# Attention with keys in tiles of 128: scores in four narrow matmuls, and half of the steps from kept score pieces that a transposing DMA turns

## The chip, the cores and the metric

One core of a Trainium2 chip runs the whole program. The metric is the device time of one execution in microseconds (us). The median of three runs of the kernel before is 2221.08 us (2217.85 to 2222.08).

## The reference

Two layers act on x of shape (4, 256, 64, 64), that is 4 batches of 256 channels by 4096 positions. Each adds its result to x and normalises its own input by groups of 8 channels first.

```python
# layer 0, on xn = group_norm(x), xf = xn as (B, 256, 4096)
f = einsum('kc,bcn->bkn', Wq, xf) + bq      # 32 channels
g = einsum('kc,bcn->bkn', Wk, xf) + bk      # 32 channels
h = einsum('oc,bcn->bon', Wv, xf) + bv      # 256 channels
s = einsum('bki,bkj->bij', f, g)            # 4096 x 4096
beta = softmax(s, axis=1)                   # over i
x = x + gamma * einsum('bci,bij->bcj', h, beta)
# layer 1, on group_norm(x)
y = relu(bn(W1 x))                          # 32 channels
z = relu(bn(W2 packed(y_i * y_j)))          # 528 pair products to 256 channels
x = x + z
```

The softmax runs over i, the positions of f (called queries in the kernel); j, the positions of g, are called keys. Every number goes through the array as float16 in a high and a low part, so one product of two split operands takes three matmuls: high by high, high by low, low by high.

## The kernel before

**Tiles.** A batch has 32 key tiles of 128 (NT) and 8 chunks of 512 queries (NCH). There are two kinds of score matmul. A piece (`step_piece`, line 1546) holds the scores of one key tile by one chunk with the keys on the partitions, in PSUM bank `tps[0]`; VectorE takes its maximum over the queries (line 801). There are 8 pieces for a key tile, 1024 in all. A step (line 1565) holds scores with the queries on the partitions: 128 queries by 512 keys (one group G), written as one matmul of 512 columns to one of two banks `sps`. The negated maxima of the group enter as three extra rows of `gst` (96 to 98): VectorE reduces them (`tile_max`), GpSimd splits them in three (`split_max`, eight small instructions, lines 1130 to 1137), TensorE turns them with four matmuls of 128 columns (`rows`, line 1572), ScalarE copies them to `gst` (`row_copy`, line 1293).

**A step** u is made in this order. TensorE writes the scores two steps ahead. ScalarE takes the exponential twice, once to float16 (`ph`, line 1300, three slots) and once to float32 (`p32`, line 1303, two slots). VectorE subtracts (`pl`, line 842). TensorE then runs 12 matmuls: for each of four key subtiles `ph` by `hth` (line 1758, 257 columns, the last one sums the powers), `ph` by `htl` (line 1759, 256 columns) and `pl` by `hth` (line 1766, 257 columns). Each subtile has its own bank `acc[0..3]`, which accumulates over the 32 steps of its group. The piece of the step 40 pieces ahead stands between the high and the low part.

**Kept steps.** From the third group of batch 0 on, one step in eight (step 4 of each eight) is kept: ScalarE copies a piece from PSUM to `ks` (line 1310), VectorE takes its maximum there (line 816) and makes a bias, ScalarE takes the exponential of `ks` twice with that bias (lines 1317, 1318), GpSimd subtracts (`kept_low`, line 1121), and a DMA issued by SP turns high and low part into `kt` (line 474). TensorE uses `kt` in lines 1725, 1726 and 1729 and needs no scores for that step. There are 120 kept and 904 made steps.

**Around it.** At the end of a group VectorE takes reciprocals of the sums and divides two of the four subtiles, ScalarE divides the other two (line 1323), and TensorE turns the result at steps 4 and 7 of the next group (`transposed`, line 1580). From batch 1 on the second layer of the batch before is woven into the steps: `rest_of_z` at step 0 of a group (7 matmuls of 512 columns, lines 1616, 1618, 1613), then ScalarE's `z_out` (line 1357) and `product_high` (line 1349), GpSimd's `low` (1098), `value_bias` (1112), `product` (1142) and `residual` (1148). Between batches `values` makes `hth` and `htl`. Ahead of the first step a prologue, in the order of the table `ORDER`, makes queries, keys and values of batch 0 and 40 pieces. The tail behind the last step is the rest of layer 1.

**Order.** Nothing is planned at run time: every engine runs its own program in order, and semaphores hold the engines together. So a wait in one engine's list also holds what stands behind it there.

Of the kernel before, what the change touches and what calls it, by code (L numbers as in the profile page):

```python
# [16 lines left out]
P = 128  # L17
CH = 512
# [14 lines left out]
KEPT_FROM = 2  # L33
KEPT = 1
TURNS_OF = (1, 2, 3, 4, 5, 0, 6, 7)
PLACES = (5,)
KEPT_STEPS = (4,)
LO = 2.0 ** 11
EXP_SHIFT = 8.0
SLOTS = 3  # L40
# [11 lines left out]
def build(nc, x, wq, wk, wv, w1, w2, vec, ident, gmean, sel, out):  # L52
# [5 lines left out]
    with ctx:  # L58
# [22 lines left out]
        p32 = sb("p32", [P, 2, CH], f32)  # L81
        ph = sb("ph", [P, SLOTS, CH], f16)
        pl = sb("pl", [P, SLOTS, CH], f16)
        mx = sb("mx", [P, NT, NCH], f32)
        nm = sb("nm", [P, QT], f32)
        mw = sb("mw", [P, 7, QT], f32)
        r1 = sb("r1", [P, QT], f32)
        r2 = sb("r2", [P, QT], f32)
        r3 = sb("r3", [P, QT], f32)
        mrow = sb("mrow", [P, QT, P], f16)  # L90
        ks = sb("ks", [P, KEPT, CH], f32)
        kb = sb("kb", [P, KEPT, 2, CH], f16)
        kt = sb("kt", [P, QT, KEPT, 2 * QT, P], f16)
        kn = sb("kn", [P, 1], f32)
        kbias = sb("kbias", [P, 1], f32)
# [61 lines left out]
        tps = [ctx.enter_context(nc.psum_tensor(f"tps{i}", [P, CH], f32)) for i in range(2)]  # L157

# [18 lines left out]
        t_mm = [sem("t_mm0"), sem("t_mm1")]  # L177
        t_free = [sem("t_free0"), sem("t_free1")]
# [9 lines left out]
        kx_ok, kn_ok, kbias_ok = sem("kx_ok"), sem("kn_ok"), sem("kbias_ok")  # L188
        kp_ok, kl_ok = sem("kp_ok"), sem("kl_ok")
        kt_in = [sem(f"kt_in{i}") for i in range(KEPT)]  # L190
        acc_mm = sem("acc_mm")
        rinv_ok = sem("rinv_ok")
        ot_act = sem("ot_act")
        ot_dve = sem("ot_dve")
# [127 lines left out]
        def z_half(n, h):  # L322

            if n >= SHARED:
                return zt[set_of(n)][:, h]
            return {(SHARED - 2, 1): p32[:, 1], (SHARED - 1, 0): ks[:, 0],
                    (SHARED - 1, 1): p32[:, 0]}.get((n, h), zt0[:])

        def rows_of(grp):
# [4 lines left out]
        ORDER = (("x", 0), ("x", 1), ("x", 2), ("qk", 0), ("x", 3), ("v", 0, 0), ("v", 0, 1), ("max", 2), ("qk", 1),  # L334
# [7 lines left out]
        AHEAD = len(EARLY)  # L342
        ALL = B * NT * NCH

        FIRST_TILE = KEPT_FROM * QT
        TILES = B * NT
        kept_fill = {}

# [1599 lines left out]
```

## Time and profile before

| | |
|---|---|
| median of three runs | 2221.08 us (2217.85 to 2222.08) |
| span of the profiled execution | 2216.6 us |
| TensorE busy | 2164.2 us, 98% |
| VectorE busy | 1857.5 us, 84% |
| ScalarE busy | 1734.7 us, 78% |
| GpSimd busy | 801.5 us, 36% |
| first attention matmul starts at | 87.7 us |

Busy time counts an instruction from its start to its modelled end, and neighbours overlap: a matmul of 257 columns is shown with 0.27 us, but one starts every 0.11 us. So for a price the start-to-start distance in the timeline is read, not the duration. The same holds for the other engines to a smaller degree (an exponential is shown with 0.69 us and the next one starts 0.57 us after it). In timeline rows an "x4" stands for four instructions merged, and the time beside it runs from the first start to the last end.

### The profile page before, as it was taken

What the parts mean: (1) busy time and instruction counts of PE and PEld (TensorE: products, weight loads), DVE (VectorE), ACT (ScalarE), POOL (GpSimd) and SP (SyncE); (2) the same over time, 40 slices, a digit from 0 to 9 for tenths busy, and PEclk for the clock granted to TensorE, in tenths of its full rate; (3) what the DMA queues carried; (4) which work ended last, traced back from release to release, by engine and by line L of the source; (5) the groups of instructions that cost most, each with busy time, mean ns of one, the idle gap of its engine ahead of it and who ended that gap; (6) DMA issues with size and microseconds to landing.
All of it is one profiled execution on the core that took longest, in us unless ns stands there. A gap on an engine that the chain in (4) does not pass through costs nothing.

```text
span 2216.6 us, 43342 instructions
## 1 busy us (share of the span) xinstructions
PE 2164.2 (98%) x16662; PEld 1607.4 (73%) x16662; DVE 1857.5 (84%) x3220; ACT 1734.7 (78%) x2806; POOL 801.5 (36%) x832
## 2 busy tenths in 40 slices
PE   4899999999999999999999999999999999999999
PEld 3577777777777777777777777777787777777754
DVE  7788888878888888888888898888988888888677
ACT  5578888878777788888777788888877778777777
POOL 2111222223233443453533344444344333343346
PEclk9999999999999999999999999999999999999999
DMA  6001111111123333322233233333212222122212
GB/s 198 14 6 20 20 26 23 27 28 28 31 60 89 82 89 80 82 64 71 62 81 85 65 83 88 89 79 85 62 35 58 61 59 53 34 50 52 62 35 76
DMA packets 186957, 132.58 MB, mean 60 GB/s; under 512 B 135520, under 2 KB 142432, under 8 KB 186720
## 3 DMA queue, kind: packets, MB, share of 16 engines
q1 hardware_dynamic: 186752, 129.81, 23.7%
q8 instruction: 132, 2.16, 0.4%
q14 instruction: 73, 0.60, 0.1%
HBM read 71.83 MB, written 19.92 MB: 41 GB/s over the span
## 4 chain that ended last, share of the span: by engine, by line
PE 90%; DVE 5%; ACT 2%; issue 1%; DMA 1%; POOL 0%; SPq 0%; ACTq 0%; POOLq 0%; DVEq 0%
PE acc L1766 16%; PE acc L1758 16%; PE acc L1759 16%; PE tps L1546 9%; PE sps L1565 8%; PE tps L1616 3%; PE acc L1540 3%; PE acc L1729 2%; PE acc L1725 2%; PE acc L1726 2%; PE tps L1618 2%; DVE mx L801 2%; PE acc L1616 1%; PE tps L1580 1%; DVE pl L842 1%
## 5 line engine op out<-in xcount | busy, mean ns | idle before, releaser
L1300 ACT ACTIVATE ph<-sps,esc 128x512 f16<-128x512 f32 x904 | 619.9, 686 | 318.7 <-PE sps L1565 312.7
L1758 PE MATMUL acc<-hth,ph 128*128 128x257 f16 x3488 | 814.7, 274 | 1.0 <-ACT ot L1323 0.9
L1759 PE MATMUL acc<-htl,ph 128*128 128x256 f16 x3488 | 813.4, 273 | 0.0
L801 DVE TENSOR_REDUCE mx<-tps 128x1 f32<-128x512 f32 x904 | 617.9, 686 | 224.4 <-PE tps L1546 214.1
L842 DVE TENSOR_TENSOR pl<-p,ph 128x512 f16<-128x512 f32 x904 | 737.3, 818 | 65.5 <-ACT p L1303 63.1
L1303 ACT ACTIVATE p<-sps,esc 128x512 f32<-128x512 f32 x904 | 616.8, 682 | 0.0
L1766 PE MATMUL acc<-hth,pl 128*128 128x257 f16 x3488 | 527.9, 273 | 0.0
L1766 PEld LDWEIGHTS acc<-hth,pl 128*128 128x128 f16 x3488 | 340.5, 98 | 134.6 <-issue 0.3
L1759 PEld LDWEIGHTS acc<-htl,ph 128*128 128x128 f16 x3488 | 341.4, 98 | 117.2 <-issue 0.3
L1546 PE MATMUL tps<-fst,gst 96*128 96x512 f16 x1024 | 390.7, 383 | 16.1 <-DVE mx L801 11.0
L1758 PEld LDWEIGHTS acc<-hth,ph 128*128 128x128 f16 x3488 | 341.1, 98 | 57.4 <-ACT ot L1323 2.7
L1121 POOL TENSOR_TENSOR kb<-ks,kb 128x512 f16<-128x512 f32 x120 | 149.0, 1241 | 596.2 <-ACT ks L1318 596.2
L1565 PE MATMUL sps<-gst,fst 128*128 128x512 f16 x904 | 343.1, 380 | 0.5 <-ACT p L1303 0.5
L1098 POOL TENSOR_TENSOR xl<-xn,xh 128x512 f16<-128x512 f32 x176 | 224.9, 1297 | 275.3 <-DVE xn L782 251.1
L1142 POOL TENSOR_TENSOR rt<-rt,yb 128x512 f32<-128x512 f32 (+1 forms) x120 | 179.0, 1523 | 42.4 <-DMA rt<-turned 42.2
L1546 PEld LDWEIGHTS tps<-fst,gst 96*128 96x128 f16 x1024 | 100.0, 98 | 50.5 <-DVE mx L801 25.5
L1130 POOL TENSOR_TENSOR r<-nm,mw 128x4 f32<-128x4 f32 x32 | 17.8, 555 | 307.7 <-DVE nm L837 307.7
L1725 PE MATMUL acc<-hth,kt 128*128 128x257 f16 x480 | 111.9, 274 | 0.0
L1726 PE MATMUL acc<-htl,kt 128*128 128x256 f16 x480 | 111.8, 273 | 0.0
L1262 ACT ACTIVATE xh<-xb,nbias,rstd 128x512 f16<-128x512 f32 x136 | 102.6, 806 | 9.3 <-DVE nbias L621 9.3
L1565 PEld LDWEIGHTS sps<-gst,fst 128*128 128x128 f16 x904 | 88.6, 98 | 28.4 <-issue 10.6
L1616 PE MATMUL tps<-qh,w2T 128*128 128x512 f16 x352 | 104.7, 379 | 0.0
(258 smaller groups left out, 2553.5 us busy)
## 6 DMA issues: line engine op xcount, KB each, us to landing
rt<-turned SPq DMA_DIRECT2D x96, 256.0 KB, 4.6
xt<-x SPq DMA_DIRECT2D x36, 512.0 KB, 3.7
xb<-x SPq DMA_DIRECT2D x32, 512.0 KB, 4.9
out<-zt SPq DMA_DIRECT2D x45, 256.0 KB, 2.7
yb<-turned SPq DMA_DIRECT2D x36, 128.0 KB, 2.6
rt<-turned SPq DMA_DIRECT2D x72, 64.0 KB, 5.0
turned<-yb SPq DMA_DIRECT2D x12, 256.0 KB, 2.4
out<-fst SPq DMA_DIRECT2D x8, 256.0 KB, 2.0
```

The source lines that it names most:

```text
L801: V.reduce_max(mx[:, tile, c:c + 1], tps[par][:], AX).then_inc(t_free[par], 1)
L842: V.tensor_tensor(pl[:, v % SLOTS], p32[:, v % 2], ph[:, v % SLOTS], ALU.subtract).then_inc(pl_ok, 1)
L1098: last = tt(xl[:, slot_of(job), h], xn[:, k % 2, h], xh[:, slot_of(job), h], ALU.subtract)
L1142: tt(rt0[0:rows, grp], rt0[0:rows, grp], yb0[0:rows, :], ALU.mult).then_inc(pb_ok, 1)
L1300: A(ph[:, v % SLOTS], sps[v % 2][:], ACT.Exp, scale=esc[:]).then_inc(ph_ok, 1)
L1303: A(p32[:, v % 2], sps[v % 2][:], ACT.Exp, scale=esc[:]).then_inc(p32_ok, 1)
L1546: fill(mm(tps[par][:], gst[0:96, key_tile(b * NT + tile)], fst[0:96, b % 2, c * CH:(c + 1) * CH], start=True, stop=True), par)
L1565: mm(sps[v % 2][:], fst[:, G // NCH % 2, tile * P:(tile + 1) * P], gst[:, keys_at(G)], start=True, stop=True).then_inc(s_mm, 1)
L1616: mm(bank[:], w2T[:, w, grp, cols], qh[k][:, grp], start=(grp == 0 and w == 0), stop=False)
L1758: mm(acc[j][:, 0:C + 1], w, hth[:, i], start=(t == 0), stop=False)
L1759: mm(acc[j][:, 0:C], w, htl[:, i], start=False, stop=False)
L1766: last = mm(acc[j][:, 0:C + 1], pl[:, v % SLOTS, j * P:(j + 1) * P], hth[:, i], start=False, stop=False)
```

## The change

The attention of a group of 512 keys over 32 tiles of 128 queries becomes the attention of one key tile of 128 over 8 chunks of 512 queries, four times per group. The number of steps stays at 1024 and each still has 12 matmuls on `hth` and `htl`, but all of them now add to one bank: `acc[0]` and `acc[1]` alternate by key tile, `acc[2]` takes the turned maxima and `acc[3]` becomes a second bank for pieces.

- **Scores** of a made step are four matmuls of 128 columns, each with weights of its own, in place of one of 512.
- **Kept steps** are 1, 3, 5 and 7 of each eight, from key tile 2 on: 504, and 520 steps are made. A kept piece goes from PSUM to `ks` on VectorE, in one instruction that also takes the maximum, in place of ScalarE's copy and VectorE's reduction. For two of the four pieces of a tile ScalarE takes both exponentials; for the other two it takes one and VectorE casts it. GpSimd's subtraction and the transposing DMA are as before, now for 504 pieces, with rings of 6 (`ks`), 3 (`kb`) and 4 (`kt`).
- **In made steps** the float32 exponential goes back to its own PSUM bank `sps` in place of `p32`; VectorE subtracts from there. `ph` has two slots. Scores are made three steps ahead behind tile 2 (two before it), and wait for `pl_ok` of the step two made steps back in place of `p32_ok`.
- **Maxima** are reduced, split, turned and copied per key tile (128 times) in place of per group (32 times). A step with s8 = 0 needs `m_ok` of its own tile; its scores stand at step 5 of the tile before.
- **Division** is all on ScalarE, at step 5 of the tile behind, after the kept powers of that place.
- **The prologue** makes 18 pieces in place of 40, and pieces are made 18 ahead in place of 40.
- **SP and GpSimd** get their orders written out by step; the waits of `transposed` at step 4 take over `y_ok`, `qk_lo` and `z_ok` waits from step 27.

```diff
-KEPT_STEPS = (4,)
+CHUNK_AT = (6, 3, 0, 4, 1, 5, 2, 7)
+KEPT_STEPS = (1, 3, 5, 7)
+FIRST_TILE = 2
+HIGH_BY_ACT = (0, 2)
+AHEAD = 18
-SLOTS = 3
+SLOTS = 2
...
+        def scored_at(w):
+            return w - 2 if w < (FIRST_TILE + 1) * NCH else w - 3
...
             def turn(tile, r):
-                sp.wait_ge(kl_ok, count_of(tile, r) + 1)
...
+                m = count_of(tile, r)
+                sp.wait_ge(kl_ok, m + 1)
+                if m >= KT_RING:
+                    sp.wait_ge(p_free, kept_step(m - KT_RING) + 1)
+                sp.dma_start_transpose(kt[:, m % KT_RING],
+                                       kb[:, m % KB_RING].rearrange("p e n -> p (e n)")).then_inc(kt_in[m % KT_RING], 16)
...
+                    V.tensor_scalar(ks[:, m % KS_RING], pbank[par][:], 1.0, None, ALU.mult, ALU.max,
+                                    accum_out=mx[:, tile % 4, PIECES[place]:PIECES[place] + 1]).then_inc(t_free[par], 1)
...
+            def kept_high(tile, r):
+                m = count_of(tile, r)
+                if r in HIGH_BY_ACT:
+                    return
+                dve.wait_ge(kp_ok, m + 1)
+                if m >= KB_RING:
+                    dve.wait_ge(*landed(m - KB_RING))
+                V.tensor_copy(kb[:, m % KB_RING, 0], ks[:, m % KS_RING]).then_inc(kc_ok, 1)
...
-                V.tensor_tensor(pl[:, v % SLOTS], p32[:, v % 2], ph[:, v % SLOTS],
+                V.tensor_tensor(pl[:, v % SLOTS], sps[v % 2][:], ph[:, v % SLOTS],
                                 ALU.subtract).then_inc(pl_ok, 1)
...
-                if v >= 2:
-                    act.wait_ge(pl_ok, v - 1)
-                A(p32[:, v % 2], sps[v % 2][:], ACT.Exp, scale=esc[:]).then_inc(p32_ok, 1)
+                A(sps[v % 2][:], sps[v % 2][:], ACT.Exp, scale=esc[:]).then_inc(p32_ok, 1)
...
# ScalarE, in attend
+                        if s8 in (3, 5, 7) and is_kept_tile(tile + 1):
+                            for r in {3: (0, 1), 5: (2,), 7: (3,)}[s8]:
+                                kept_powers(tile + 1, r)
+                        if s8 == 5:
+                            if t > 5 or J:
+                                divide(tile - 1)
+                            if tile + 1 < TILES:
+                                row_copy(tile + 1, acc[2])
...
# GpSimd, in its main loop
+                        if t % NCH in (2, 4, 5, 7) and is_kept_tile(tile):
+                            kept_low(tile, (2, 4, 5, 7).index(t % NCH))
+                        if t % NCH == 7 and tile + 1 < TILES:
+                            split_max(tile + 1)
...
+                        if t >= 27 and b:
+                            product(n, t - 27)
...
             def scores(u):
-                v = made(u)
+                v, tile, c = made(u), u // NCH, CHUNK_AT[u % NCH]
                 if v >= 2:
-                    pe.wait_ge(p32_ok, v - 1)
...
-                mm(sps[v % 2][:], fst[:, G // NCH % 2, tile * P:(tile + 1) * P], gst[:, keys_at(G)], start=True,
-                   stop=True).then_inc(s_mm, 1)
...
+                    pe.wait_ge(pl_ok, v - 1)
+                if u % NCH == 0:
+                    pe.wait_ge(m_ok, tile + 1)
                 for q in range(QT):
...
+                    at = c * CH + q * P
+                    last = mm(sps[v % 2][:, q * P:(q + 1) * P], fst[:, tile // NT % 2, at:at + P],
+                              gst[:, key_tile(tile)], start=True, stop=True)
+                last.then_inc(s_mm, 1)
...
             def transposed(G, h, par):
-                pe.wait_ge(ot_act, 2 * (G + 1))
-                pe.wait_ge(ot_dve, 2 * (G + 1))
+                pe.wait_ge(ot_act, QT * (G + 1))
```

## Rows read from the trace of the kernel before

**Rows 1.** Page, parts 1 and 2: TensorE's busy time, and its granted clock.

```profile
PE 2164.2 (98%) x16662; PEld 1607.4 (73%) x16662; DVE 1857.5 (84%) x3220; ACT 1734.7 (78%) x2806; POOL 801.5 (36%) x832
...
PEclk9999999999999999999999999999999999999999
```

**Rows 2.** Page, part 4: the chain that ended last, by engine.

```profile
PE 90%; DVE 5%; ACT 2%; issue 1%; DMA 1%; POOL 0%; SPq 0%; ACTq 0%; POOLq 0%; DVEq 0%
```

**Rows 3.** Groups by line: shapes xcount | busy us, mean ns | idle before <-releaser.

```profile
L1758 PE MATMUL acc<-hth,ph 128*128 128x257 f16 x3488 | 814.7, 274 | 1.0 <-ACT ot L1323 0.9
...
L1565 PE MATMUL sps<-gst,fst 128*128 128x512 f16 x904 | 343.1, 380 | 0.5 <-ACT p L1303 0.5
```

**Rows 4.** Timeline, TensorE around a `rows` (start us, us of the merged instructions).

```profile
1161.84 0.38 PE L1546 MATMUL tps<-fst,gst 96*128 96x512 f16 x1
1162.06 0.60 PE L1766 MATMUL acc<-hth,pl 128*128 128x257 f16 x4
1162.50 0.39 PE L1572 MATMUL tps<-idh,mrow 128*128 128x128 f16 x4
1162.73 0.38 PE L1565 MATMUL sps<-gst,fst 128*128 128x512 f16 x1
1162.94 0.27 PE L1725 MATMUL acc<-hth,kt 128*128 128x257 f16 x1
```

**Rows 5.** Timeline, TensorE: the low part of a kept step.

```profile
1181.13 0.61 PE L1729 MATMUL acc<-hth,kt 128*128 128x257 f16 x4
1181.58 0.38 PE L1565 MATMUL sps<-gst,fst 128*128 128x512 f16 x1
```

**Rows 6.** Who waited for whom: engine line <- releaser: us in total, times, longest.

```profile
PEld tps L1546 <- DVE mx L801: 25.5, 63, 1.5
...
PE tps L1546 <- DVE mx L801: 11.0, 28, 1.4
```

**Rows 7.** Timeline, VectorE and ScalarE before the first step (brackets: idle before, releaser).

```profile
72.41 4.92 DVE L801 TENSOR_REDUCE mx<-tps 128x1 f32<-128x512 f32 x8
...
77.47 0.19 DVE L837 TENSOR_REDUCE nm<-mx 128x4 f32<-128x32 f32 x1
...
79.20 0.60 ACT L1289 ACTIVATE hth<-acc 128x512 f16<-128x512 f32 x1 [7.62 <-PE acc L1540]
```

**Rows 8.** Timeline, ScalarE at the start of a group of batch 2.

```profile
1172.99 0.78 ACT L1357 ACTIVATE zt<-tps,t,sc 128x512 f32<-128x512 f32 x1
...
1175.32 0.68 ACT L1303 ACTIVATE p<-sps,esc 128x512 f32<-128x512 f32 x1
1175.89 0.63 ACT L1349 ACTIVATE qh<-rt 128x512 f16<-128x512 f32 x1
1176.41 0.81 ACT L1317 ACTIVATE kb<-ks,kbias,esc 128x512 f16<-128x512 f32 x1
1177.12 0.80 ACT L1318 ACTIVATE ks<-ks,kbias,esc 128x512 f32<-128x512 f32 x1
```

**Rows 9.** Timeline, TensorE at that start: `rest_of_z` begins.

```profile
1171.27 0.59 PE L1616 MATMUL tps<-qh,w2T 128*128 128x512 f16 x2
```

**Rows 10.** Groups by line, VectorE and GpSimd (columns as in rows 3).

```profile
L842 DVE TENSOR_TENSOR pl<-p,ph 128x512 f16<-128x512 f32 x904 | 737.3, 818 | 65.5 <-ACT p L1303 63.1 <-issue 0.2
...
L1121 POOL TENSOR_TENSOR kb<-ks,kb 128x512 f16<-128x512 f32 x120 | 149.0, 1241 | 596.2 <-ACT ks L1318 596.2
...
L796 DVE TENSOR_TENSOR htl<-acc,hth 128x512 f16<-128x512 f32 x58 | 39.0, 683 | 15.6 <-ACT hth L1289 15.5
...
L1130 POOL TENSOR_TENSOR r<-nm,mw 128x4 f32<-128x4 f32 x32 | 17.8, 555 | 307.7 <-DVE nm L837 307.7
```

**Rows 11.** Stages: us, busy (x) of PE, PEld, DVE, ACT, POOL, PEclk, DMA share, GB/s.

```profile
150.00:300.00 150.00, 149.54 (x1195) 115.81 (x1194) 129.82 (x257) 122.32 (x199) 28.72 (x39) 1.00 0.10 19
...
800.00:1000.00 200.00, 200.00 (x1553) 147.72 (x1551) 173.35 (x282) 163.25 (x265) 87.35 (x83) 1.00 0.31 79
```

**Rows 12.** DMA issues: line, queue, op xcount, us to landing.

```profile
kt<-kb SPq DMA_TRANSPOSE x120, 3.0
```

More of the change, by code:

```diff
@@ L353, in kept_before, with made, step_of @@
-        def kept_before(t):
-            return KEPT * (t // NCH) + sum(e < t % NCH for e in KEPT_STEPS)
-        def queries_of(u):
-            t = u % NT
-            return t if u // NT < KEPT_FROM else KEPT * QT + t - kept_before(t)
+            return u // NCH >= FIRST_TILE and u % NCH in KEPT_STEPS
+        MADE = [u for u in range(ALL) if not kept(u)]
+        MADE_AT = {u: v for v, u in enumerate(MADE)}
+        def made(u):
+            return MADE_AT[u]
+        def step_of(v):
+            return MADE[v]
@@ L371, in build, with casts_until, kept_step @@
-        MADE = [u for u in range(B * STEPS) if not kept(u)]
-        def step_of(v):
-            return MADE[v]
-        def tile_at(u, place):
-            tile = (u + AHEAD - place) // NCH
-            return tile if (u + AHEAD - place) % NCH == 0 and FIRST_TILE <= tile < TILES else None
-        def tile_before(u, place):
-            return tile_at(u - NCH, place)
+        def casts_until(m):
+            return sum(k % KEPT not in HIGH_BY_ACT for k in range(m + 1))
+        def kept_step(m):
+            return NCH * (FIRST_TILE + m // KEPT) + KEPT_STEPS[m % KEPT]
@@ L818, in kept_bias @@
[L818 to L837 removed]
+                    par, r = piece_bank(u + AHEAD), place - (NCH - KEPT)
@@ L1152, in _ @@
                 low(("first", 0, c))
-            split_max(0)
+            for tile in range(2):
+                split_max(tile)
             for b in range(B):
@@ L1768, in attend @@
-                        if not kept(u):
-                            last.then_inc(p_free, 1)
+                        if s8 == 0 and t == 0 and J == 0 and b:
+                            pe.wait_ge(h_lo, 2 * G + 12)
+                        elif s8 == 0 and tile >= 2:
+                            pe.wait_ge(ot_act, tile - 1)
+                        for q in range(QT):
+                            mm(bank[:, 0:C + 1], high[:, q], hth[:, c * QT + q], start=(s8 == 0 and q == 0), stop=False)
+                            mm(bank[:, 0:C], high[:, q], htl[:, c * QT + q], start=False, stop=False)
@@ new lines, in attend @@
+                        if (J, t) == (0, 0) and b:
+                            pe.wait_ge(h_lo, 2 * (G + NCH))
+                        if (b, J, t) == (0, 0, 1):
+                            pe.wait_ge(h_lo, 2 * NCH)
+                        step_piece(u)
+                        if not kept(u):
+                            pe.wait_ge(pl_ok, v + 1)
+                        for q in range(QT):
+                            last = mm(bank[:, 0:C + 1], low[:, q], hth[:, c * QT + q], start=False,
+                                      stop=(s8 == NCH - 1 and q == QT - 1))
@@ L1770, in attend @@
+                        last.then_inc(p_free, 1)
+                        if s8 == 2 and tile + 1 < TILES:
+                            rows(tile + 1, acc[2])
                         if b == 0 and (J, t) in ((1, 18), (1, 21), (2, 9)):
```

502 lines of the change are left out of this document (203 added, 299 removed), and 9 rows, old and new, of the table ORDER.

## The prediction

> **What bounds the kernel now.** I read the page first: TensorE is busy 98% of the span at a granted clock of 9 tenths or more in every slice [rows 1], and it holds 90% of the chain that ended last [rows 2]. Busy time of overlapping matmuls can hide waits, so next the groups: the matmuls of the steps have next to no idle time before them [rows 3]. Then the stages: from 800 to 1000 us TensorE is busy for the whole 200 us, VectorE for 173, ScalarE for 163, GpSimd for 87 [rows 11]. So TensorE's instruction stream is the time from the first step to the last, and the other engines have 13 to 56% to spare. The stream is priced by distances of starts in the timeline, all at the high level of the clock (2.4 GHz): a piece 0.22 us (1161.84 to 1162.06), a matmul of 257 columns 0.11 (four in 1162.06 to 1162.50), a score matmul of 512 columns 0.21 (1162.73 to 1162.94, rounded down; with the piece's 0.22 I take 0.216), and one of 128 columns 0.057 (four in 1162.50 to 1162.73) [rows 4]. A made step costs 0.22 + 0.216 + 12 x 0.11 = 1.76 us, a kept one 1.54.
>
> **The change, part by part.**
>
> *Scores.* Before, 904 x 0.216 = 195.3 us. After, 520 steps x 4 x 0.057 = 118.6 us, if four narrow matmuls, each with its own weights, run as the four of `rows` do. That row is just this pattern (128 rows by 128 columns, float16, new weights each time), and the four loads hid. Term: -76.7 us, on the path. The Trainium skill, "TensorE: Matmul & The Clock Gate", section Back-to-back issue gap, gives about 81 ns for each load and matmul of 128 columns in a sustained stream; by that estimate the scores cost 168.5 us and the term is -26.8. Its 131 ns for 512 columns lies far from the 0.216 above, so by this trace I keep 57.
>
> *Low parts.* Four matmuls of 257 columns that add to one bank take 0.45 us in a kept step (1181.13 to 1181.58) [rows 5], against 0.44 over four banks [rows 4]. All steps now have one bank: 904 x about 0.006 us (the rows allow 0 to 0.02) = +5 us, bounds 0 and +18. The high parts of a kept step also add to one bank; they cost nothing more in the kernel before.
>
> *Waits of the pieces for VectorE.* Before, one bank is refilled each step; TensorE and its loads wait 11.0 and 25.5 us for the maxima, in part the same waits and in part in the prologue [rows 6]. With two banks VectorE gets a step (1.6 us) more. I take -10 us, bounds 0 and -18 (half of the sum).
>
> *Prologue.* 22 pieces fewer. Eight maxima take 4.92 us in a row, and `tile_max` comes only behind them; ScalarE then stood 7.62 us waiting for value matmuls that were queued behind these pieces [rows 7]. 22 x 0.61 = 13.5 us of VectorE go from a stretch where it is what is waited for. But the 22 pieces aren't dropped, they are made later among steps: +22 x 0.22 = 4.8 us. Net -9, bounds 0 (the projections' own chain of ScalarE and transfers is as long) and -12. The steps without a piece at the end are 18 in place of 40; that is the same 4.8 us.
>
> *ScalarE.* Exponentials of a made step start 0.57 us apart, those on `ks` 0.70, `product_high` takes 0.52 [rows 8]. Per eight steps: before 14 x 0.57 + 2 x 0.70 + the copy, about 10 us; after 8 x 0.57 + 6 x 0.70 = 8.8 us plus a division and a row copy (fewer columns than a product, so at most 0.5 each), 9.8 us of at least 13.2. In sum hidden. Not hidden, I think, is one place, since its list is in order. At the start of a group (batches 1 to 3) ScalarE waits in `z_out` for `rest_of_z`, which lands 1.72 us after its first matmul (1171.27 to 1172.99) [rows 8, 9]. Behind it stand: `z_out` 0.78, kept powers 0 and 1 (3 x 0.70), a product 0.52, two powers 1.14, a product 0.52, kept powers 2 (1.40), the division 0.5: done at 1.72 + 6.96 = 8.7 us. TensorE wants the division at step 4 (`transposed`): 7 x 0.216 + 1.54 + 1.77 + 1.54 + 0.06 + 1.77 = 8.2 us. It stalls some 0.5 us, in the 20 groups that have all of this: +10 us. Bounds 0 (if the list runs that much faster) and +25 (1.25 us each).
>
> *VectorE.* A kept piece costs one pass in place of a reduction elsewhere; the low part reads PSUM, as line 796 does, 683 ns against a mean of 818 [rows 10]. The accumulating copy isn't in the trace: between 683 and, with one small instruction more to read the accumulator (0.19 us for `nm` [rows 7]), 873; I take 720. Per eight steps: 4 plain maxima 2.4, 4 accumulating copies 2.9, 4 low parts 2.7, two casts at the same 0.68 each, small ones 0.7: 10.1 of 13.2 us. Hidden, cost 0; without cover a step would grow by what exceeds 1.65 us.
>
> *GpSimd* gets 504 x 1.24 us of subtractions in place of 120 [rows 10], and 128 x 8 small instructions in place of 32 x 8. In the stage at 800 us it is busy 87.35 of 200 us [rows 11]. A group of that stage lasts about 64 us (28 made and 4 kept steps 55.4; 26 matmuls of the second layer 5.6; projections and transposes some 2.8, an estimate from their counts), a new one 16 x 1.77 + 16 x 1.54 + 8.4 = 61.4. So GpSimd has 27.9 us in an old group; less 4 x 1.24 and one split, plus 16 x 1.24 and four splits (eight instructions of at most 0.56 us [rows 10], 3.0 us as an estimate), it is 51.7 of 61.4 us. Its order puts each `kept_low` 7 or 8 steps (12 us) before use, a transfer takes 3.0 us from issue to landing [rows 12]. Cost 0; see the third rival.
>
> *Transfers.* From 150 to 300 us the DMA engines are busy 0.10 of the time, with about ten transposing transfers in it (four a group) [rows 11]: at most 1.5 us each of all 16. 504 of them take 760 us of 2140, beside 0.2 to 0.3 for the rest. Not a bound. SP only issues them, one per two steps.
>
> *Maxima.* 128 matmuls of 128 columns as before. `rows` of the next tile stands at step 2, its copy is wanted at the start of step 5: 3.3 us for a matmul and a short copy. Hidden while ScalarE isn't behind; +4 us for this and other places I can't name, bounds 0 and +15.
>
> **The sum**, against the profiled execution, whose span of 2216.6 lies 4.5 us below the median: -76.7 + 5 - 10 - 9 + 10 + 4 = -76.7. Span 2140, time 2144 us.
>
> **Rivals.**
> 1. *The other lists keep clear too* (stalls of step 4 and of the maxima stay away, the pieces' waits go fully, the prologue gives 12): -76.7 + 0 - 18 - 12 = -107, 2114 us. For it: the spare time in [rows 11]. Against: the list above is 0.4 us too long by the rows.
> 2. *The in-order lists of ScalarE and VectorE bite in every tile*, not only at group starts: `row_copy` stands behind kept powers and a division, and if it comes 0.4 us late in 126 tiles, that gives +50: 2190 us. For it: ScalarE has two fixed points per tile, the scores and the `rows`. Against: 9.8 of 13.2 us are filled.
> 3. *GpSimd becomes the bound.* Every kept piece passes it, in order, behind ScalarE's power or VectorE's cast; each wait there adds to the 51.7 us of its group. From (61.4 - 51.7) / 16 = 0.6 us of wait per piece on it sets the pace; at 0.8 us (64.5 us, 3.1 over, 24 groups) the gain is used up; at 0.9 us a group takes 66.1 us, 4.7 over, +113: 2257 us, slower than before. For it: the 596 us that it waits before `kept_low` now [rows 10] show that it stands where it must wait. Against: those waits are slack of an idle engine; the queue runs ahead by whole steps only when it isn't filled. The rule of the Trainium skill, "SBUF — State Buffer", section Who interferes with whom, that a VectorE instruction with two SBUF inputs holds off a GpSimd one that reads SBUF, would relieve it here, since the new low part has one SBUF input; the mean of 818 against 683 fits that.
> 4. *Narrow loads don't hide* in this place, and each matmul waits for a load of 96 ns (1607.4 us of loads over 16662 [rows 1]): 4 x 96 = 384 ns in place of 228, 520 x 0.156 = +81: 2225 us, a little slower than before. Against: [rows 4] show the opposite. With half of that effect (77 ns a matmul) it is 2185. The skill's 81 ns (above) would give 2194.
>
> **How the numbers follow.** Main case 0.55; rival 1 0.13; rival 2 0.17; rival 3 0.07; rival 4 in full 0.02, in half 0.06. Faster by over 0.2% (about what a measurement here can tell from none, 4.4 us) are all but rival 3 and the full rival 4: 0.91; same 0.02; slower 0.07. The range: the main case with its bounds reaches from 2114 (all its bounds on the low side, which is rival 1) to 2180 (low parts +18, `transposed` +25 and the other terms as taken give 2172, some of the rest 2180). That alone would leave out rivals 2, 3 and 4, 0.32; taken up to rival 2's time it is 2114 to 2190 and leaves out about 0.2.
>
> **What the profile after would show.** Scores: starts 0.056 to 0.058 us apart in the new score line; 0.08 or more means rival 4. First step at 72 to 76 us. `transposed` waits for the division some 20 times, about 0.5 us each. GpSimd about 70% busy, and TensorE waiting for `kt` nowhere; waits for landings or for `gst` in every tile would mean rival 3 or 2. No line of pieces waits for VectorE any more. The prediction is wrong if TensorE's busy share falls below some 96%, or the group of 64 us doesn't come out near 61.

## The result, and the profile after

The changed kernel takes 2256.0 us (median of 4, 2251.5 to 2259.4) where the kernel before takes 2219.7 (2217.9 to 2222.1): ratio 1.0162, 95% interval 1.0146 to 1.0178. It is 36 us slower; 2144 was forecast, 2114 to 2190 the range. The profiled execution has a span of 2257.5 us, 40.9 more than before.

The page answers to [rows 1] and [rows 2]:

```profile
span 2257.5 us, 48571 instructions
...
PE 2120.5 (94%) x17838; PEld 1650.4 (73%) x17838; DVE 1622.7 (72%) x3479; ACT 1598.3 (71%) x2594; POOL 1285.1 (57%) x1984
...
PE 60%; ACT 9%; issue 9%; DMA 8%; SPq 6%; POOL 4%; DVE 4%; ACTq 0%; DVEq 0%; POOLq 0%
```

TensorE alone is no longer the bound. It fell from 98 to 94% (below 96, the prediction's own sign of being wrong), VectorE and ScalarE fell too, GpSimd is at 57%, and the chain of work, 90% TensorE before, is TensorE for 60% and goes through ScalarE, transfers (DMA) and SyncE's issues (SPq) for much of the rest. Two stages of 200 us, with the columns of [rows 11] (length, busy us of PE, PEld, DVE, ACT, POOL with counts, granted clock, DMA share, GB/s):

```profile
300.00:500.00 200.00, 194.84 (x1760) 160.10 (x1758) 148.93 (x334) 148.23 (x240) 104.80 (x187) 1.00 0.45 83
1000.00:1200.00 200.00, 189.92 (x1610) 150.57 (x1608) 147.03 (x310) 143.01 (x234) 121.90 (x179) 0.97 0.55 111
```

In batch 0 (300 to 500 us) TensorE is idle for 5 of 200 us (0.7 in the same stretch before). From 1000 to 1200 us, across the border of batches 1 and 2, it is idle for 10 (2.1 before) and also shows a granted clock of 0.97 (1.00 before). Who waited for whom (engine line <- what ended the wait: us in total, times, longest), the counterpart of [rows 6]:

```profile
POOL kb L1115 <- DVE kb L839: 548.6, 239, 7.2
...
ACT kb L1297 <- DMA kt<-kb: 127.4, 58, 6.5
...
PE sps L1545 <- ACT gst L1280: 47.4, 21, 4.4
...
DVE kb L839 <- DMA kt<-kb: 41.2, 19, 3.2
...
PE tps L1560 <- ACT ot L1305: 17.8, 20, 2.7
```

Three places are new. TensorE's scores wait for the row copy (L1280) 21 times, 2.3 us on average. `transposed` waits 20 times for the division (L1305). And ScalarE in the exponentials of kept pieces ("kept powers", L1297) and VectorE in the casts (L839) wait for the landing of a transposing transfer, which is what frees a slot of the `kb` ring.

One of the 21, in batch 1, step 21 of a group. TensorE, then ScalarE, then SyncE's issues:

```profile
1059.94 0.61 PE L1730 MATMUL acc<-hth,pl 128*128 128x257 f16 x4
1063.83 0.58 PE L1545 MATMUL sps<-gst,fst 128*128 128x128 f16 x4 [3.28 <-ACT gst L1280]
1064.21 0.42 PE L1720 MATMUL acc<-hth,kt 128*128 128x257 f16 x1
```

```profile
1056.49 0.65 ACT L1288 ACTIVATE sps<-sps,esc 128x512 f32<-128x512 f32 x1
1061.51 0.81 ACT L1297 ACTIVATE kb<-ks,kbias,esc 128x512 f16<-128x512 f32 x1 [4.38 <-DMA kt<-kb]
1062.23 0.80 ACT L1299 ACTIVATE ks<-ks,kbias,esc 128x512 f32<-128x512 f32 x1
1062.94 0.45 ACT L1305 ACTIVATE ot<-acc,rinv 128x256 f32<-128x256 f32 x1
1063.41 0.27 ACT L1280 ACTIVATE gst<-acc 3x128 f16<-3x128 f32 x1
```

```profile
1048.88 1.18 SPq L468 DMA_DIRECT2D yb<-turned  x2
1050.11 2.00 SPq L471 DMA_DIRECT2D rt<-turned  x4
1052.15 1.36 SPq L474 DMA_DIRECT2D rt<-turned  x3
1053.61 0.40 SPq L430 DMA_DIRECT2D xt<-x  x1
1054.12 4.80 SPq L482 DMA_TRANSPOSE kt<-kb  x2
```

The first of these last two transfers, in the chain of work:

```profile
1054.12 7.31 DMA kt<-kb
```

Read backwards: TensorE stands 3.3 us for the row copy, 0.27 us of work on three rows. The row copy stands in ScalarE's list behind a division and the third kept power; that one waited 4.4 us for a landing. The landing took 7.3 us instead of the usual 3.1, and its issue came behind nine plain transfers of the second layer (`rotate`) and a load of x (`xt`, 512 KB), which occupied SyncE from 1048.88 to 1054.0. GpSimd had finished this piece at 1051.1, so of a landing some 7.2 us late, 3.0 us are the late issue and 4.2 the longer way from issue to landing. After the pause TensorE's matmuls are spaced 0.21 us instead of 0.11, and the granted clock from 1063.8 to 1067.0 us is 0.50: the lower of its two levels (1.2 GHz). In the stretches in which the trace shows that level, 229 matmuls of all shapes between 88 and 2172 us start at about double distance, which costs 25 us; before there were 8 of them, 1 us.

TensorE's stalls can be counted as the time by which its starts lie further apart than usual, added up by step number modulo 32 over all groups; time at the lower clock is in it. This gives about 129 us, before about 18. Some 34 us lie at step 21 and 26 at step 29 (scores behind the row copy), 23 at step 4 (division), 27 at steps 31 and 0 (pieces, whose banks VectorE holds while its cast waits for a landing), 11 at 22 and 30 (low clock after a stall). Odd chunks issue `rotate` at step 14 and stall at 21, even ones issue at 21 and stall at 29.

The balance from the first to the last attention step is 2040.8 us before and 2085.5 after, +44.7: scores -78.8 (904 x 0.216 against 2080 x 0.056), 22 pieces moved in +4.8, low parts +8, stalls +111 add up to +45.

### The profile page after: what moved, and what is told of

It reads as the page before. It is cut to its first block, busy times and chain, and to the rows that moved or that the text cites. A ratio compares the mean times of both kernels' runs of the same rounds, so it can differ in the third digit from the quotient of the medians.

```text
span 2257.5 us, 48571 instructions
## 1 busy us (share of the span) xinstructions
PE 2120.5 (94%) x17838; PEld 1650.4 (73%) x17838; DVE 1622.7 (72%) x3479; ACT 1598.3 (71%) x2594; POOL 1285.1 (57%) x1984
## 4 chain that ended last, share of the span: by engine, by line
PE 60%; ACT 9%; issue 9%; DMA 8%; SPq 6%; POOL 4%; DVE 4%; ACTq 0%; DVEq 0%; POOLq 0%
PE acc L1730 13%; PE acc L1720 12%; PE acc L1721 12%; DMA kt<-kb 7%; PE sps L1545 3%; PE tps L1525 3%; PE acc L1525 3%; PE acc L1519 3%; POOL kb L1115 3%; PE tps L1596 3%; ACT ks L1299 3%; ACT kb L1297 2%; PE acc L1596 1%; PE tps L1560 1%; PE tps L1598 1%
## 5 line engine op out<-in xcount | busy, mean ns | idle before, releaser
L1115 POOL TENSOR_TENSOR kb<-ks,kb 128x512 f16<-128x512 f32 x504 | 593.3, 1183 | 628.0 <-DVE kb L839 548.6
L844 DVE TENSOR_TENSOR pl<-sps,ph 128x512 f16<-128x512 f32 x520 | 356.7, 686 | 251.4 <-ACT sps L1288 251.1
L1287 ACT ACTIVATE ph<-sps,esc 128x512 f16<-128x512 f32 x520 | 355.4, 684 | 223.1 <-PE sps L1545 209.5
L1720 PE MATMUL acc<-hth,ph 128*128 128x257 f16 x2080 | 491.6, 276 | 0.0
L1721 PE MATMUL acc<-htl,ph 128*128 128x256 f16 x2080 | 490.8, 275 | 0.0
L1720 PE MATMUL acc<-hth,kt 128*128 128x257 f16 x2016 | 475.5, 276 | 0.0
L1721 PE MATMUL acc<-htl,kt 128*128 128x256 f16 x2016 | 475.2, 275 | 0.0
L1299 ACT ACTIVATE ks<-ks,kbias,esc 128x512 f32<-128x512 f32 x504 | 393.8, 807 | 0.0
L1288 ACT ACTIVATE sps<-sps,esc 128x512 f32<-128x512 f32 x520 | 339.8, 653 | 0.0
L1730 PE MATMUL acc<-hth,pl 128*128 128x257 f16 x2080 | 320.4, 275 | 0.0
L1730 PE MATMUL acc<-hth,kt 128*128 128x257 f16 x2016 | 312.8, 277 | 0.0
L1297 ACT ACTIVATE kb<-ks,kbias,esc 128x512 f16<-128x512 f32 x252 | 204.3, 811 | 127.9 <-DMA kt<-kb 127.4
L1545 PE MATMUL sps<-gst,fst 128*128 128x128 f16 x2080 | 202.5, 220 | 53.4 <-ACT gst L1280 47.4
```

The lines of the kernel that those rows point to most:

```text
L844: V.tensor_tensor(pl[:, v % SLOTS], sps[v % 2][:], ph[:, v % SLOTS], ALU.subtract).then_inc(pl_ok, 1)
L1115: tt(kb[:, m % KB_RING, 1], ks[:, m % KS_RING], kb[:, m % KB_RING, 0], ALU.subtract).then_inc(kl_ok, 1)
L1287: A(ph[:, v % SLOTS], sps[v % 2][:], ACT.Exp, scale=esc[:]).then_inc(ph_ok, 1)
L1288: A(sps[v % 2][:], sps[v % 2][:], ACT.Exp, scale=esc[:]).then_inc(p32_ok, 1)
L1297: A(kb[:, m % KB_RING, 0], ks[:, m % KS_RING], ACT.Exp, bias=kbias[:, tile % 2:tile % 2 + 1], scale=esc[:])
L1299: A(ks[:, m % KS_RING], ks[:, m % KS_RING], ACT.Exp, bias=kbias[:, tile % 2:tile % 2 + 1], scale=esc[:]).then_inc(kp_ok, 1)
```

## The experiments

Ratios below stand against the kernel before on the same chip (medians of 2218.2 to 2219.7 us there); brackets hold the 95% interval. Three theories were named beforehand. A, the order: in ScalarE's list the third kept power, which waits for a landing, stands ahead of the division and the row copy. B, the supply: transfers or GpSimd can't feed the rings. C: ScalarE's list is too long.

### The order of ScalarE's list

```diff
-    for r in {3: (0, 1), 5: (2,), 7: (3,)}[s8]:
+    for r in {3: (0, 1), 5: (), 7: (3,)}[s8]:
 ...
     row_copy(tile + 1, acc[2])
+    if is_kept_tile(tile + 1):
+        kept_powers(tile + 1, 2)
```

> The changed kernel, with one order altered on ScalarE: at step 5 of a tile the division and the row copy come before the kept powers of piece 2, not behind them. Nothing is left out. Theory A (the order): in the changed kernel ScalarE stands in kept powers 2 until a transposing transfer has landed and freed its kb slot (127 us in 58 waits), and the row copy behind it makes TensorE wait at steps 21 or 29 (about 60 us, and 11 more at the low clock behind it) and the division at step 4 (23 us). Then these waits go: about 2256 - 80 = 2175 us, below the kernel before. Theory B (the supply): the transfers and GpSimd can't keep up with 504 pieces, and any order only moves the wait: to ph at steps 22 and 30 or to kt; 2240 us or more, with TensorE's idle time as large as before. Theory C (ScalarE's list is simply too long): the waits at steps 21 and 29 turn into waits for ph of about the same length, 2230 us or more, and ScalarE shows no idle time before line 1297.

Measured: 2217.6 us, 0.9996 (0.9984 to 1.0009). 38 us gained, not 80. The scores no longer wait for the copy, but the next thing in the list does:

```profile
L1722 PE MATMUL acc<-hth,ph 128*128 128x257 f16 x2080 | 487.8, 275 | 16.7 <-ACT ph L1287 16.5
```

The kept power, still at step 5, holds off the made power of step 6. So it was moved behind that one:

```diff
-if s8 in (3, 5, 7) and is_kept_tile(tile + 1):
-    for r in {3: (0, 1), 5: (2,), 7: (3,)}[s8]:
+if s8 in (3, 6, 7) and is_kept_tile(tile + 1):
+    for r in {3: (0, 1), 6: (2,), 7: (3,)}[s8]:
```

> As the run before, with the kept powers of piece 2 one step later still, behind the powers of step 6. Nothing is left out. Theory A: what ScalarE waits for then stands behind one more instruction pair that TensorE needs, so another 0 to 15 us less than with the row copy first: 2165 us. Theory B: no better than the run before, perhaps worse, since the low part and the transfer of piece 2 start later; 2240 or more. Theory C: same as the run before.

Measured: 2185.2 us, 0.9856 (0.9837 to 0.9876). Where one pair of instructions stands in one list is worth 71 us. The line of `ph`, and ScalarE's waits for landings:

```profile
L1720 PE MATMUL acc<-hth,ph 128*128 128x257 f16 x2080 | 486.7, 274 | 0.4 <-ACT ph L1287 0.4
```

```profile
ACT kb L1297 <- DMA kt<-kb: 68.0, 37, 6.5
```

Landings did not get faster: of the 504 transposing transfers 42 took over 5 us, 39 in the changed kernel. The long waits are still there, with less of what others need behind them. ScalarE's list has the same length, which speaks against C.

### The rings

```diff
-KS_RING = 6
-KB_RING = 3
+KS_RING = 5
+KB_RING = 4
```

> The changed kernel with a ring of 4 for kb (3 before) and of 5 for ks (6 before); there is no room for more. The order is untouched, nothing is left out. If the wait is for the kb slot, as theory A says, kept powers 2 then need the landing of the piece before the one they wait for now, and ScalarE's waits for landings fall from 127 us to under 40; the stalls at 21 and 29 mostly go, the one at step 4 (which is ScalarE's own list, 0.6 us each at least) stays at some 12 us: 2195 us, if the shorter ks ring costs nothing. Theory B: the wait comes back on kt or on the ks ring, 2250 us. Theory C: 2250 us.

Measured: 2204.5 us, 0.9934 (0.9919 to 0.9949). 52 us, with the order left alone. ScalarE's waits for landings fall from 127.4 to 28.0 us, as foreseen, and the stalls at 21 are gone. Those at step 4 (12 us) and a part of those at 29 stay. At step 30 of the first group of a batch there are new ones, some 22 us: the shorter `ks` ring isn't free. VectorE, which fills it, waited 23.0 us in 6 times for GpSimd in the changed kernel and does so more here:

```profile
ACT kb L1297 <- DMA kt<-kb: 28.0, 12, 4.7
...
DVE ks L811 <- POOL kb L1115: 52.9, 28, 9.8
```

Both together:

> Both mendings at once: the third kept exponential a step later, behind the division and the row copy (2185 us alone), and a ring of four result buffers and five piece buffers instead of three and six (2204 us alone). With the order, the stalls left are at pieces (steps 24, 31 and 0), where VectorE waits for a transfer; a fourth buffer takes these out. Order and supply as independent causes: 2256 - 71 - 52 would be 2133, but each took partly the same stalls, so I expect 2165 to 2175. If the fourth buffer adds nothing once the order is mended (2183 or more), supply was never a cause of its own.

Measured: 2180.7 us, 0.9831 (0.9816 to 0.9846), outside the 2165 to 2175 that were expected. It is 5 us better than the order alone, hardly clear of the noise (the intervals touch): both edits remove mostly the same stalls, and the shorter `ks` ring brings its own. That one was left, 17.7 us at step 30 of the first group of batches 1 to 3. VectorE and GpSimd there:

```profile
616.90 0.69 DVE L811 TENSOR_SCALAR_CACHE_REDUCE ks<-tps 128x512 f32<-128x512 f32 x1 [7.20 <-POOL kb L1115]
```

```profile
614.40 1.26 POOL L1136 TENSOR_TENSOR rt<-rt,yb 128x512 f32<-128x512 f32 x1 [9.54 <-DMA rt<-turned]
615.62 1.15 POOL L1115 TENSOR_TENSOR kb<-ks,kb 128x512 f16<-128x512 f32 x1
```

VectorE waits 7.2 us for a `ks` slot, which GpSimd's subtraction has to free, which stands behind a product that waits 9.5 us for the channels that `rotate` brings.

### GpSimd's list

The products of these groups go three steps later:

```diff
-if t >= 27 and b:
-    product(n, t - 27)
+if b and J and t >= 27:
+    product(n, t - 27)
+if b and not J and t >= 30:
+    product(n, t - 30)
+if b and J == 1 and t <= 2:
+    product(n - 1, t + 2)
```

> e4_late_kb4 with one more thing moved: in the first group of batches 1 to 3 GpSimd's five products, which wait for the turned channels, go from steps 27 to 31 to steps 30, 31 and the first three of the next group. In e4_late_kb4 TensorE stands at step 30 of these three groups for 4.8 to 6.7 us, 17.7 us in all, for a piece bank; the chain that I read is: piece bank held by VectorE, whose copy waits for a free piece buffer, which GpSimd's subtraction has to free, and that stands in its list behind the product, which waits for the plain transfers issued at step 25. If this is right, the 17.7 us go: 2163 us (2160 to 2168). If GpSimd simply has too much work there, moving it frees nothing: 2178 to 2185.

Measured: 2163.5 us, 0.9746 (0.9731 to 0.9760), as expected. Its page shows a TensorE-bound kernel again:

```profile
PE 2090.3 (97%) x17838; PEld 1640.1 (76%) x17838; DVE 1641.0 (76%) x3479; ACT 1592.5 (74%) x2594; POOL 1291.8 (60%) x1984
...
PE 81%; DVE 7%; ACT 4%; issue 3%; POOL 2%; SPq 1%; DMA 1%; DVEq 0%; ACTq 0%; POOLq 0%
```

Two runs take one of its three edits (order, rings, products) back each. First the rings:

> The same two moves (third kept exponential a step later, products of the first groups later), but with the rings of the changed kernel, three result buffers and six piece buffers. Supply theory: with only three result buffers ScalarE and VectorE wait again for landings, 2175 us. Order theory: rings matter little once no list stands in the wrong place, 2165 us.

Measured: 2179.2 us, 0.9815 (0.9798 to 0.9831). The order theory alone is refuted here: with the old rings (three slots of `kb`, six of `ks`) 16 us come back, at pieces (steps 0, 24) and at `transposed`.

Then the order:

> e8_late_product (2163 us) with the third kept exponential back at step 5, ahead of the division and the row copy; rings of four and five and the later products stay. If the order of ScalarE's list is a cause of its own, the waits of TensorE for the division at step 4 (20 times 0.6 us) and for the row copy come back: in e4 against e2 the same edit was worth 24 us, so 2187 us (2180 to 2195). If the fourth result buffer already gives all the slack and the order was only another way to it: 2168 or less.

Measured: 2181.9 us, 0.9837 (0.9823 to 0.9852). The order is worth 18 us of its own. Some 13 of them are at step 4, where `transposed` waits for the division in 21 groups again (once in e8_late_product), and about 7 are scores waiting at step 29:

```profile
PE tps L1564 <- ACT ot L1309: 9.6, 21, 0.8
```

So order and rings are each a cause, and they overlap. The runs side by side (us):

| order mended | rings 4 and 5 | products later | time |
|---|---|---|---|
| no | no | no | 2256.0 |
| yes | no | no | 2185.2 |
| no | yes | no | 2204.5 |
| yes | yes | no | 2180.7 |
| yes | no | yes | 2179.2 |
| no | yes | yes | 2181.9 |
| yes | yes | yes | 2163.5 |

All three give 93 us; the order alone gives 71 of them and the rings alone 52. The later products give 6 us with the old rings and 17 with the new ones, so a good part of what they repair came with the shorter `ks` ring. Products alone were not run.

The last reading, a residual that holds GpSimd at steps 20 to 24 of the last groups:

```diff
-if t == 20 and b and 1 <= n < SHARED - 1:
+if t == (24 if J == NCH - 1 else 20) and b and 1 <= n < SHARED - 1:
     residual(n - 1, 0)
```

> e8_late_product with GpSimd's residual of the last group of batches 1 to 3 moved from step 20 to step 24 (its store from 22 to 26). In e8_late_product TensorE stands at steps 23 and 24 of these groups, 1.4 and 2.1 us each, behind a chain piece bank, VectorE's copy (3.07 us of waiting), GpSimd's subtraction, which stands behind this residual. By that reading 3 to 10 us go: 2154 to 2160. If another instruction of the list takes its place, nothing: 2163.

Measured: 2160.4 us, 0.9747 (0.9731 to 0.9763). Its median is 3 us lower and its ratio the same; whether it gains anything is not decided.

### Is GpSimd's load a bound?

```diff
-tt(kb[:, m % KB_RING, 1], ks[:, m % KS_RING], kb[:, m % KB_RING, 0], ALU.subtract).then_inc(kl_ok, 1)
+for i in range(4):
+    at = slice(i * P, (i + 1) * P)
+    last = tt(kb[:, m % KB_RING, 1, at], ks[:, m % KS_RING, at], kb[:, m % KB_RING, 0, at], ALU.subtract)
+last.then_inc(kl_ok, 1)
```

> e8_late_product with each of GpSimd's 504 subtractions split in four of 128 columns: the same bytes, three more fixed costs, an estimated 0.6 us more of GpSimd per kept piece, 300 us in all. My third rival put the point from which GpSimd decides at 0.6 us per piece. If GpSimd is near that point, its list now delays the transfers: above 2200 us. If it has room (57 percent busy in the changed kernel), the time stays below 2175.

Measured: 2166.9 us, 0.9772 (0.9757 to 0.9786), with

```profile
PE 2089.5 (97%) x17838; PEld 1640.0 (76%) x17838; DVE 1614.6 (75%) x3479; ACT 1592.0 (74%) x2594; POOL 1532.1 (71%) x3496
```

240 us more work on GpSimd (0.48 per kept piece, below the estimate of 0.6) cost 3 to 6 us. In the mended kernel, then, GpSimd's load is far from being the bound; the changed kernel itself was not run with it.

### The plain transfers beside the transposing ones

First with few bytes:

```diff
-sp.dma_start(yb0[2 * MID * i:2 * MID * (i + 1)], turned[n % 2]).then_inc(rot_in, 16)
+sp.dma_start(yb0[2 * MID * i:2 * MID * (i + 1), 0:16], turned[n % 2, :, 0:16]).then_inc(rot_in, 16)
```

The transfers to `rt0` likewise (16 of 512 columns; the rest of the turned channels is left out, so the second layer works on other numbers):

> The changed kernel with the transfers that turn layer 1's channels (rotate) cut to 16 of 512 columns; their number and their place in SP's list stay, so layer 1 multiplies stale data. Theory A has two halves: SP issues nine transfers, some 5.5 us, ahead of the next transposing one, and their bytes (1.4 MB) then lie ahead of it on the DMA engines, so that it lands after 7.3 us and not 3.1. If the bytes are the larger half, the stalls at 21 and 29 fall by more than half: 2215 us. If SP's issuing is, they stay within a third: 2240 us. Theory C: no change, 2256 us.

Measured: 2208.5 us, 0.9956 (0.9941 to 0.9972). 12 transposing transfers over 5 us instead of 39, none over 6.5 instead of 6, and 48 us. SyncE's issues take as long as before (0.42 to 0.57 us each), and the waits of the scores for the row copy fall from 47.4 to 15.6 us,

```profile
PE sps L1546 <- ACT gst L1281: 15.6, 11, 3.1
```

so the bytes are the larger half. ScalarE's own waits for landings fall less, from 127.4 to 90.4 us. Two things are mixed in with the 48 us. GpSimd's products, whose input is this transfer too, wait 21.9 us in place of 47.0. And the profiled execution starts its first step at 80.0 us in place of 84.5, which the edit doesn't explain.

The trace of the changed kernel says the same of the landings. 87 transposing transfers were issued beside transfers of `rotate` (from 6 us behind one to 4 us ahead of one): 4.4 us in the median, 31 over 5 us. 109 stood beside a load of x of 512 KB alone: 3.1 us, 8 over 5 us. Of the other 308 none took over 5 us. All 12 long ones of e3_small_turns stood beside such a load, so those loads go with late landings too, if less often.

Then the issues spread, one or two per step, with the order mended:

```diff
-if t == 14 and b and n % 2:
-    rotate(n)
+if b and n % 2 and t in ROTATE[1]:   # two at 16 and 24, one at 14, 18, 19, 20, 22
+    rotate(n, ROTATE[1][t])
```

(even chunks likewise from 21 to 26; in the first group of a batch, one at 25 and the rest at 26)

> The third kept exponential a step later (2185 us alone), and the nine plain transfers that turn a chunk's channels no longer issued in a row by SyncE but one or two per step between the transposing ones, from step 14 (odd chunks) or 21 (even chunks) on. If the late landings (7.3 us against 3.0) come from standing behind that burst, the stalls at steps 24 and 29 (16 us) and part of those at 0 go: 2165 to 2175. If they come from the bytes as such, wherever these stand, nothing is gained: 2182 or more.

Measured: 2214.1 us, 0.9979 (0.9968 to 0.9990), 29 us slower than the order alone. Landings over 5 us: 38, against 42 with the order alone and 39 in the changed kernel. A new wait took over:

```profile
POOL rt L1146 <- DMA rt<-turned: 135.4, 22, 12.6
```

The channels now arrive late, GpSimd stands in its products (48 us in e1b_copy_first_late), the subtractions behind it too, and TensorE stalls 34 us at step 31 of even chunks.

Then the same transfers from another engine:

```diff
-sp.dma_start(yb0[2 * MID * i:2 * MID * (i + 1)], turned[n % 2]).then_inc(rot_in, 16)
+nc.gpsimd.dma_start(yb0[2 * MID * i:2 * MID * (i + 1)], turned[n % 2]).then_inc(rot_in, 16)
```

(and all others of `rotate`, with its waits)

> The changed kernel with the plain transfers that turn a chunk's channels issued by GpSimd instead of SyncE, at the same steps; bytes and shapes are the same, the transposing transfers stay with SyncE. If the landings of 7.3 us come from standing behind these transfers in one queue, they fall to 3 to 4 us and the stalls at steps 21 and 29 (60 us) mostly go: 2200 to 2215, unless issuing costs GpSimd more than SyncE. If they come from the bytes on the shared DMA engines, the landings stay at 6 to 8 us and the time at 2245 or more.

Measured: 2353.5 us, 1.0601 (1.0584 to 1.0617). Landings over 5 us: 26 instead of 39, the longest 10.4 us. It doesn't separate the two cleanly, since issuing holds GpSimd:

```profile
PEld acc L1554 <- POOL mrow L1109: 111.0, 21, 10.0
```

TensorE's `rows` now wait for `split_max`, which stands behind the issues in GpSimd's list, 105 us in 21 waits. What can be said: issuing the plain transfers from another engine does not remove the long landings, fewer bytes do for the most part, spreading the issues doesn't.

### The price of the narrow scores, and the tiling alone

In the kernel before:

```diff
-mm(sps[v % 2][:], fst[:, G // NCH % 2, tile * P:(tile + 1) * P], gst[:, keys_at(G)], start=True,
-   stop=True).then_inc(s_mm, 1)
+at = keys_at(G)
+for q in range(QT):
+    last = mm(sps[v % 2][:, q * P:(q + 1) * P], fst[:, G // NCH % 2, tile * P:(tile + 1) * P],
+              gst[:, at.start + q * P:at.start + (q + 1) * P], start=True, stop=True)
+last.then_inc(s_mm, 1)
```

> The kernel before, whose scores of each step are written in four matmuls of 128 columns instead of one of 512; nothing else is changed. It measures the price of the narrow score matmul by itself. The trace of the changed kernel shows them 56 ns apart, so four take 224 ns where one took 216: by that 1026 steps cost about 8 us, 2227 us. If the narrow weight loads did not hide (my fourth rival), each step would cost 80 to 110 ns more, 2300 us or above. The other theories (order of ScalarE's list, late transfers) say nothing of this run.

Measured: 2224.7 us, 1.0027 (1.0016 to 1.0038), +6. The kernel has 904 made steps, not the 1026 of the expectation, so 904 x 8 ns = 7 us was due. Rival 4 is refuted, in full and in half (half of it would be 904 x 0.08 = 72 us here).

```profile
L1567 PE MATMUL sps<-gst,fst 128*128 128x128 f16 x3616 | 349.8, 219 | 0.5 <-ACT p L1303 0.5
```

And the changed kernel with no kept step:

```diff
-FIRST_TILE = 2
+FIRST_TILE = 128
```

> The changed kernel with its first kept tile set past the last, so that every step has its scores computed and none is turned by a transfer: the new tiling alone. It needs 8 us more of score matmuls than before. If what the changed kernel loses all lies in the kept steps (both of my theories: order of ScalarE's list, and late transfers), it comes out at 2225 to 2235 us with stalls of TensorE no larger than before's 18 us. If the new tiling itself (its prologue, its row copy at step 5, the transposes at step 4) makes the stalls, it comes out above 2245.

Measured: 2520.6 us, 1.1360 (1.1341 to 1.1379). By its letter the second branch came true (above 2245), but not at the places that it names: the expectation overlooked a loop. The float32 power goes back into the score bank, so a bank is free for new scores only behind two powers and a subtraction. Where every step is made, that sets the pace (the chain):

```profile
1102.71 0.69 ACT ph L1287
1103.40 0.56 ACT sps L1288
...
1103.98 0.70 DVE pl L844
...
1104.73 0.40 PE sps L1545 x4
```

The exponential at 1102.71 had waited 2.2 us for TensorE to finish the step two before, whose `ph` slot it needs (two slots in place of three), and that closes the loop. Such waits are 713.8 us here and 9.2 in the changed kernel:

```profile
ACT ph L1287 <- PE acc L1730: 713.8, 797, 3.2
```

Kept steps between the made ones give the loop its time. So this run does not tell what the tiling alone costs; it tells that the tiling, with its powers in the score bank and two slots, needs the kept steps. Which of the two matters more was not tested.

## Why the prediction was wrong, point by point

- **What bounds the kernel before**: right; the argument that everything is TensorE's stream held for that kernel.
- **Scores** (-76.7): right. The new score line follows its neighbours at 56 ns, 0.22 us for four in the changed kernel's chain, and 2080 of them cost 116.5 us, a term of -78.8:

```profile
1045.71 0.22 PE sps L1545 x4
1045.93 0.11 PE acc L1720
```

  The 81 ns that the Trainium skill gives ("TensorE: Matmul & The Clock Gate", Back-to-back issue gap) are not what this trace shows.
- **Low parts** (+5): a little small. Four take 450 ns in the median where they took 442, +8 us over 904 steps; within the bounds.
- **Waits of the pieces** (-10): wrong sign. VectorE got a wait for a landing and one for a `ks` slot, and the banks stay full behind it. Pieces start late by some 27 us at steps 31 and 0. Over all steps it is about 26 us even in e8_late_product, against 14 before. No run shows what the second bank is worth by itself.
- **Prologue** (-9): wrong. First step at 84.5 us, not 72 to 76; with +4.8 for the moved pieces the net is +1.6. One profile doesn't fix that number: in the profiles of the experiments on the changed kernel the first step starts between 80.0 and 87.2 us (e3, e9), before at 87.7 and in e7 at 90.0. None is near 76. I took VectorE's maxima for the bound because they stood in the trace. Behind them is a chain per chunk: four issues of SyncE (0.5 to 0.6 us each where they don't wait), a landing, piece, projection. The prediction's bound of 0 named it. After it the third step's scores, which now wait for the subtraction of the first, stand ahead of the first step (TensorE waits 2.6 us there). Both, in the changed kernel's chain:

```profile
68.73 1.21 SPq L440
69.98 1.83 DMA gst<-zt
...
83.42 0.70 DVE pl L844
84.12 0.14 issue
84.25 0.38 PE sps L1545 x4
```

  No experiment was made on the prologue.
- **`transposed` at step 4** (+10): right in place and count (20), 23 us instead of 10, within its bounds. The landing waits are the surplus: with the fourth `kb` slot (e2) the waits fall from 17.8 us to 9.6 in 21 times.
- **ScalarE** ("In sum hidden. Not hidden, I think, is one place"): here is the step that failed. The sum was right (71% busy, 9.8 of 13.2 foreseen), and the one place that I priced was found by adding up durations. I gave the list's waits no price beyond `rest_of_z`. The third kept power waits for the landing of the kept piece three before it (`landed(m - KB_RING)`), and behind it in the list stand the division and the row copy. The kernel before has such a wait too (line 1316), but for one piece in eight steps, and its waits show none for `kt<-kb`. After, it is 127.4 us in 58 waits. The forecast's room of 12 us for a transfer of 3.0 us was reckoned for the use of `kt`, not for the slot of `kb`. Moving the kept power gave 71 us back, a fourth slot 52.
- **VectorE**: durations right (the accumulating copy takes 685 + 80 ns with its read; I took 720; the low part 686). Its list has the same flaw at the cast, which waits 41.2 us for landings.
- **GpSimd**: right that its load fits, as e11_more_gpsimd shows, though the load was put too high (forecast 70%, measured 57 to 60). The subtraction takes 1183 ns on average, not 1240, and the small instructions of `split_max` 190 to 292 ns each, not up to 560. Wrong as "cost 0": its list stands behind the product, which was worth 6 us with the changed kernel's rings.
- **Transfers** ("not a bound", 3.0 us to landing): right in the median, 3.1 us (504 of them, page's part 6),

```profile
kt<-kb SPq DMA_TRANSPOSE x504, 3.1
```

  but I took one median for a resource with a tail. [rows 12] is from a kernel with 120 such transfers, of which one took over 5 us. The share was foreseen at some 0.55 to 0.65 and is 0.51.
- **Maxima** (+4, bounds to +15): failed, about 60 us at steps 21 and 29. Rival 2 had this mechanism (row copy behind kept powers and a division, scores late) at 0.4 us in 126 tiles; the profile shows 0.7 to 4.4 us in 21 tiles. It was the nearest rival; its size was missed because it was priced as a busy list and not as a list that stands.
- **Rival 3** gave about the time, 2257, by luck: its reason, GpSimd as the bound, does not hold.

With the three edits the forecast comes near: -54 us of span instead of -76.7. The 22 us between are roughly these: the prologue 9, the low parts 3, and the pieces 22, which wait 12 us more instead of 10 less; against them some 10 us of `transposed` that are not lost, and 2 us by which the scores came out better.

## What to carry to other kernels

When a change puts a wait into an in-order list, or makes one come more often, write down everything behind it on that engine and who needs it next, and price the wait by the worst landings, found where transfers crowd, not by the median. Instructions of 0.3 us that another engine is waiting for go ahead of long ones that wait for a ring slot. Ring depth and order repaired partly the same stall here, so their gains did not add up. A busy share that falls on the engine that was the bound, and a chain spread over several engines, were the sign of this fault; moving two kinds of instructions in their lists, with one slot more for `kb` and one less for `ks`, turned +36 us into -56.

## What was not expected of the hardware

- A transposing transfer of 256 KB lands in 3.1 us in the median of 504, but in 7.3 us, the longest, next to about 2 MB of plain transfers (two of 128 KB, four of 256, three of 64, one of 512); 39 took over 5 us, 12 when those of `rotate` carried a thirty-second of their bytes (e3_small_turns).
- Four matmuls of 128 columns with new weights each cost only 8 ns more than one of 512 (224 against 216), confirmed by +6 us in 904 steps.
- Four low-part matmuls of 257 columns take 450 ns when they add to one bank and 442 over four banks. The high parts, 257 and 256 columns by turns, also add to one bank now and start 109 to 110 ns apart as before, so one bank alone is not the whole reason; what is stays open.
- After pauses such as the one of 3.3 us above TensorE went on at 1.2 GHz (granted clock 0.50, matmuls 0.21 us apart): 25 us in the whole kernel against 1 before.
- Splitting GpSimd's subtraction of 512 columns (1.18 us) in four takes 0.48 us more (e11_more_gpsimd).
